# The order in which two lanes' steps are merged on each engine, and the numbers of constant products, laid out once more in a chain of eight attention and feed-forward stages

## Chip, cores and metric

One core of one Trainium2 chip. The metric is the device time of one execution in microseconds.

## What is computed

32 samples of 128 tokens by 128 features go through four layers, each a gated cross-attention and a gated feed-forward, in fp32:

```
x = x + tanh(g_xattn[l]) * attention_l(norm(x), ctx)
x = x + tanh(g_ffn[l])   * ffn_l(norm(x))
```

- Layer 0: attention with 16 heads of 8; a mixture of 8 experts, top 2, and 2 shared ones.
- Layer 1: causal attention with 16 heads; a "switched" attention as feed-forward: 8 value and output experts for each head, top 2 chosen by a token's own gates on the value side and on the output side.
- Layer 2: an mLSTM (4 heads, exponential gates, cumulated logarithms of the forget gates); a feed-forward of ternary weights with a convolution of width 3 in between.
- Layer 3: a wide attention with 16 heads and a feed-forward of its own; a mixture of 16 experts.

## The kernel before

The weights stay in SBUF. The samples are worked in 8 turns (counted from 0) of 2 lanes of 2 samples (G = 2). A lane goes through eight stages in each turn: A0 (small attention), M0 (mixture), A1 (small attention), SW (switched attention), ML (mLSTM), CF (feed-forward with convolution), WA (wide attention), M3 (second mixture). Every engine runs both lanes, so that one lane has work where the other waits.

What each engine does for a lane is written as a generator (pe_lane, act_lane, dve_lane, pool_lane, sp_lane) that yields between its steps ("chunks"). On each engine weave() (line 135) merges the two generators into one stream of instructions: a chunk n of a turn t of lane k has the number t * TURN + BEATS[k][n], and the chunk with the lower number is issued first. The numbers do nothing else; the waits on semaphores stay within the chunks. Each turn of a lane has 173 chunks on TensorE and 22 on SyncE. Engines run in order, so a chunk whose semaphore is not up holds the other lane's chunks behind it.

```
while heads:
    head = min(heads, key=lambda h: h[:2])
    ...
    turn, chunk = divmod(n + 1, len(beats[k]))
    head[0], head[2] = turn * TURN + beats[k][chunk], n + 1
```

spare() (line 334) issues so many products of a constant bf16 identity (L336), into a bank that is written afterwards anyway, as the next number in SPARES says: 101 calls a lane and turn, each ahead of a wait of TensorE. Their results are used by nobody.

The lines that the prediction goes by:

- SyncE, sp_lane: for each lane the switched attention stores its values to DRAM and reloads them in another layout: pv_d (store L1784, load L1788), the mixing matrix mix_d (store L1792, load L1795), v_d (store L1800, load L1804), the selection sel_d (L1807, L1810) and the outputs o_d (store L1816, load L1819), one for each sample, in 22 chunks with a wait each. The inputs of the next turn and the output of this are chunks 20 and 21.
- ScalarE: spread (L949) makes the mixing weights from what mix_d's load brought; keep_values (L954) takes the mixed values out of PSUM for v_d; L942 spreads q and k; L862 and L869 are the attentions' exponentials and copies.
- TensorE: L344 turns the normed x; L408, L431 and L440 end a small attention; L532, L535 and L544 are the projections of the switched attention, L559 its scores, L574 its mixed values, L589 its attention's product with the values, L603 and L616 its outputs; L685 and L693 are in the mLSTM.
- VectorE: L1202 takes the maximum of scores; L1369 finishes the mixing matrix that mix_d's store waits for.

Of the kernel before, what the change touches and what calls it, by code (L numbers as in the profile page):

```python
# [49 lines left out]
), (  # L50
# [11 lines left out]
))  # L62
BEATS_ACT = ((
# [7 lines left out]
), (  # L71
# [7 lines left out]
))  # L79
BEATS_DVE = ((  # L80
# [10 lines left out]
), (  # L91
# [10 lines left out]
))  # L102
BEATS_POOL = ((
    47832, 55688, 59143, 64674, 67070, 70207, 71015, 77823, 79861, 83113, 84484,
# [1827 lines left out]
```

## Time and profile before

| what | us |
|---|---|
| median of three runs (lowest, highest) | 2446.69 (2446.49, 2448.3) |
| the profiled execution | 2447.47 |
| its span, first to last instruction | 2445.4 |
| TensorE busy | 2223.2 |
| VectorE busy | 1749.4 |
| ScalarE busy | 1290.7 |
| mean granted clock of TensorE | 0.976 |

The profiled execution is 0.8 us above the median; 2.1 us of it lie outside the span. Busy shares add up over stages with different limits, so the table alone does not say what holds a stage: the rows below do, by stretch.

### The profile page before, as it was taken

Reading aid. Unit: us, or ns where it says so; the run is one execution under the profiler, and the core shown is the slowest. Engines: PE = TensorE matmul, PEld = TensorE weight load, DVE = VectorE, ACT = ScalarE, POOL = GpSimd, SP = SyncE. Lnnn points to the kernel's source line nnn. Section 1 sums busy time; section 2 is a strip of 40 time slices with the busy share of each in tenths; the row PEclk is TensorE's granted clock in tenths of the full one; section 3 lists DMA queues with packets and bytes.
Section 4 is the critical chain, followed back from the end, with each engine's and each line's share of the span. In section 5 each row is a group of like instructions: output and inputs, shape, how many; then the busy total and the mean of one; then the engine's idle time right before and its main releaser. Section 6 shows DMA issues by size and latency. Waiting matters only on the chain.

```text
span 2445.4 us, 51545 instructions
## 1 busy us (share of the span) xinstructions
PE 2223.2 (91%) x19938; PEld 1612.2 (66%) x19938; DVE 1749.4 (72%) x5567; ACT 1290.7 (53%) x3714; POOL 141.2 (6%) x180
## 2 busy tenths in 40 slices
PE   7899989989899998999899988999889998899998
PEld 3668657676567765677666766667666676666766
DVE  6874787757877577774877758777587775877657
ACT  4366354664547545474444744547344473445734
POOL 0000100001000010000100010000110001100010
PEclk9999999999999899998999999999899998999989
DMA  4034000340004300042000520006100061000610
GB/s 172 1 88 104 9 14 1 96 96 10 14 1 113 79 9 14 1 122 70 9 14 1 129 63 9 14 1 147 45 18 6 2 156 36 20 3 13 151 29 5
DMA packets 312516, 115.52 MB, mean 47 GB/s; under 512 B 268752, under 2 KB 295376, under 8 KB 312016
## 3 DMA queue, kind: packets, MB, share of 16 engines
q1 hardware_dynamic: 312272, 112.23, 17.9%
q8 instruction: 158, 2.59, 0.4%
q14 instruction: 86, 0.70, 0.1%
HBM read 63.96 MB, written 48.23 MB: 46 GB/s over the span
## 4 chain that ended last, share of the span: by engine, by line
PE 49%; DVE 30%; ACT 8%; DMA 5%; issue 4%; POOL 3%; SPq 1%; DVEq 0%; ACTq 0%
PE banks L450 7%; PE banks L386 6%; PE banks L589 3%; PE banks L505 3%; ACT PP L862 3%; PE banks L616 3%; PE banks L383 2%; PE banks L336 2%; DVE nm L1202 2%; DVE qk L1283 2%; DMA mix_d<-gs 2%; PE banks L544 2%; PE banks L397 2%; PE banks L559 2%; POOL mv L1741 2%
## 5 line engine op out<-in xcount | busy, mean ns | idle before, releaser
L862 ACT ACTIVATE PP<-banks,nm 128x128 f32<-128x128 f32 x1568 | 443.7, 391 | 210.8 <-DVE nm L1202 120.5
L1202 DVE TENSOR_REDUCE nm<-banks 128x4 f32<-128x512 f32 (+1 forms) x400 | 261.3, 675 | 136.3 <-PE banks L386 100.7
L336 PE MATMUL banks<-identb 128*128 128x256 bf16 x1840 | 289.1, 277 | 16.4 <-ACT PP L1017 8.5
L450 PE MATMUL banks<-w_sb,PP 128*128 128x128 f32 x1536 | 247.8, 285 | 45.7 <-ACT PP L862 17.6
L450 PEld LDWEIGHTS banks<-w_sb,PP 128*128 128x128 f32 x1536 | 167.4, 142 | 122.9 <-issue 64.0
L336 PEld LDWEIGHTS banks<-identb 128*128 128x128 bf16 x1840 | 177.2, 101 | 106.6 <-issue 48.0
L1741 POOL TENSOR_TENSOR mv<-mv,half 128x2 f32<-128x2 f32 x160 | 113.0, 706 | 2135.0 <-DVE mv L1099 2135.0
L1245 DVE COPY PP<-banks 128x512 f32<-128x512 f32 x256 | 175.8, 689 | 61.1 <-PE banks L450 60.2
L505 PE MATMUL banks<-w_sb,qk 128*128 128x128 f32 x1280 | 180.6, 280 | 2.0 <-DVE qk L1346 1.3
L505 PEld LDWEIGHTS banks<-w_sb,qk 128*128 128x128 f32 x1280 | 164.7, 194 | 20.1 <-issue 11.4
L386 PE MATMUL banks<-qk,gs 32*128 32x512 f32 x512 | 147.5, 653 | 0.0
L589 PE MATMUL banks<-va,PP 128*128 128x128 f32 x1024 | 139.3, 282 | 2.3 <-DVE oa L1391 2.3
L589 PEld LDWEIGHTS banks<-va,PP 128*128 128x128 f32 x1024 | 124.6, 194 | 8.5 <-DVE oa L1391 4.2
L853 ACT ACTIVATE xnT<-banks 128x256 f32<-128x256 f32 x128 | 49.1, 384 | 149.0 <-PE banks L344 149.0
L544 PE MATMUL banks<-xnT,w_sb 128*128 128x256 f32 x512 | 121.0, 384 | 0.6
L916 ACT ACTIVATE tmp<-banks 128x256 f32<-128x256 f32 x160 | 60.5, 383 | 103.1 <-PE banks L475 102.3
L544 PEld LDWEIGHTS banks<-xnT,w_sb 128*128 128x128 f32 x512 | 94.0, 190 | 25.4 <-issue 7.7
L397 PE MATMUL banks<-PP,va 128*32 128x128 f32 x2048 | 102.8, 284 | 3.9 <-DVE PP L1245 3.9
L1346 DVE TENSOR_TENSOR qk<-qk,banks 128x256 f32<-128x256 f32 x256 | 96.2, 416 | 8.2 <-PE banks L498 4.4
L1114 DVE TENSOR_SCALAR xn<-x,mv 128x128 f32<-128x128 f32 x256 | 76.7, 342 | 34.0 <-POOL mv L1741 32.6
L474 PE MATMUL banks<-xnT,w_sb 128*128 128x256 f32 x320 | 97.9, 388 | 0.5 <-DVE wstat L1700 0.5
L475 PE MATMUL banks<-xnT,w_sb 128*128 128x256 f32 x320 | 95.6, 381 | 0.0
(283 smaller groups left out, 4267.4 us busy)
## 6 DMA issues: line engine op xcount, KB each, us to landing
va<-v_d SPq DMA_DIRECT2D x32, 512.0 KB, 3.8
o_d<-oa SPq DMA_DIRECT2D x64, 256.0 KB, 4.2
va<-o_d SPq DMA_DIRECT2D x32, 512.0 KB, 4.4
pv_d<-PP SPq DMA_DIRECT2D x32, 256.0 KB, 2.0
oa<-pv_d SPq DMA_DIRECT2D x32, 256.0 KB, 3.2
v_d<-PP SPq DMA_DIRECT2D x16, 512.0 KB, 4.0
v_d<-tmp SPq DMA_DIRECT2D x16, 512.0 KB, 4.4
w_sb<-weights SPq DMA_DIRECT2D x1, 5599.0 KB, 24.2
```

The costliest lines, as they stand in the source:

```text
L336: pe.matmul(bank(k, n)[:, cols(c, T)], identb[:, :], bc(identb[:, :], 1, G), start=True, stop=True, skip_group_check=True)
L386: pe.matmul(bank(k, c), qT[k][rows, cols(b)], km[rows, b, :], start=False, stop=True, skip_group_check=True).then_inc(s_ps[k], 1)
L397: e = pe.matmul(bank(k, 3)[32 * j:32 * j + 32, cols(g)], v4[:, b, HQ * g + j, :], PT[k][:, 512 * (u % 2) + 128 * j:][:, 0:128], start=True ...
L450: e = pe.transpose(bank(k, 2)[:, cols(j)], P[k][:, 512 * (u % 2) + 128 * j:][:, 0:128], ident)
L474: pe.matmul(hb[:, 0:T], w("w1_0", n * 128, (n + 1) * 128), xnT[k][:, :], start=True, stop=True)
L505: e = pe.matmul(bank(k, 0)[:, cols(b)], qk[k][:, n * T + b * 128:n * T + (b + 1) * 128], w(weight, n * 128, (n + 1) * 128), start=n == 8 a ...
L544: pe.matmul(bank(k, n % 4)[:, 0:T], w(("sq1", "sk1")[n % 2], n // 2 * 128, (n // 2 + 1) * 128), xnT[k][:, :], start=True, stop=True).then_ ...
L589: e = pe.matmul(bank(k, 3)[:, cols(j)], PT[k][:, 512 * (u % 2) + 128 * j:][:, 0:128], va3[k][:, n:G * H + 1:G * H - n, :], start=True, sto ...
L862: e = act.activation(P[k][:, 512 * (u % 2) + 128 * j:][:, 0:128], bank_[:, cols(j)], ACT.Exp, bias=nm[k][:, m:m + 1])
L1202: e = dve.tensor_reduce(m, b3(scores[:, 0:maps * 128], maps), AX.X, ALU.max, negate=True)
L1245: dve.tensor_copy(PT[k][:, cols(n % 2, 512)], bank(k, 2)).then_inc(pT_ok[k], 1)
L1741: pool.tensor_tensor(a, a, half[:, 0:n], ALU.pow).then_inc(pw[k], 1)
```

## The change

Only the numbers in BEATS_PE, BEATS_ACT, BEATS_DVE, BEATS_POOL and BEATS_SP, and in SPARES, are others. TURN stays at 39873. No instruction but the constant products is added or removed.

```diff
 BEATS_PE = ((
-    -1250, -612, -326, -44, 358, 653, 679, 1059, 1283, 1395, 1454, 1561, 1923, 2116, 2199, 2211, 2316, 2889, 2917, 2958,
...
+    0, 468, 605, 752, 1234, 1691, 1757, 2193, 2482, 2548, 2703, 2769, 3076, 3291, 3570, 3618, 3684, 4085, 4462, 4528, 4653,
...
 BEATS_SP = ((
-    -242752, -242553, -242553, -238131, -238131, -237804, -237804, -237058, -236981, -233923, -230618, -221598, -219346,
-    -218796, -217615, -212325, -212215, -209270, -206607, -206485, -203699, -203699,
+    16795, 16911, 17360, 17410, 17765, 17815, 17945, 18356, 18920, 19533, 20031, 20850, 21669, 22414, 22463, 22704, 23055,
+    23779, 24239, 24662, 36199, 39918,
 ), (
-    -235003, -231213, -230164, -229008, -229008, -228143, -225901, -221262, -221262, -221262, -221262, -218853, -213790,
-    -209157, -209065, -206564, -205345, -205168, -204765, -204680, -203168, -203066,
+    18840, 19064, 19405, 19455, 19810, 19860, 19953, 20364, 20693, 21228, 21390, 22209, 23145, 23730, 24298, 24539, 24890,
+    24980, 25641, 26064, 39969, 57767,
 ))
...
 SPARES = (
-    3, 1, 0, 0, 1, 0, 0, 0, 0, 0, 0, 0, 0, 0, 0, 0, 0, 0, 0, 1, 7, 0, 8, 0, 3, 0, 0, 0, 0, 0, 0, 0, 0, 0, 0, 0, 4, 0, 0, 0,
-    0, 0, 0, 0, 0, 2, 1, 0, 5, 0, 0, 1, 5, 0, 0, 0, 0, 0, 0, 0, 0, 0, 0, 0, 0, 0, 0, 0, 0, 0, 1, 0, 0, 0, 0, 2, 1, 3, 8, 3,
-    0, 9, 8, 0, 0, 0, 3, 0, 0, 2, 2, 3, 4, 0, 3, 8, 0, 9, 3, 1, 0,
+    7, 0, 0, 0, 1, 0, 0, 0, 2, 0, 0, 0, 0, 0, 0, 1, 0, 0, 0, 1, 1, 0, 11, 0, 2, 0, 1, 0, 0, 0, 0, 0, 5, 0, 0, 0, 1, 0, 0, 0,
+    0, 0, 0, 0, 0, 1, 0, 0, 3, 0, 3, 0, 2, 3, 0, 0, 0, 0, 0, 0, 0, 0, 0, 0, 0, 0, 3, 0, 0, 0, 3, 0, 0, 0, 0, 0, 2, 3, 7, 2,
+    0, 7, 4, 0, 0, 0, 7, 0, 0, 1, 3, 0, 3, 0, 2, 9, 0, 3, 5, 8, 0,
 )
```

Merging both sets of numbers by weave()'s rule gives these orders (lane.chunk):

- SyncE, one turn, before: 0.20 0.21 1.20 1.21 0.0 to 0.8, 1.0, 0.9, 1.1, 0.10, 1.2 to 1.6, 0.11, 1.7 to 1.10, 0.12, 1.11, 0.13, 0.14, 1.12, 0.15, 0.16, 0.17, 1.13, 1.14, 0.18, 1.15, 0.19, 1.16 to 1.19 (the first four are of the turn before). After: 0.20 0.21 1.20 0.0 to 0.5, 1.21, 0.6, 0.7, 1.0, 0.8, 1.1, 1.2, 1.3, 0.9, 1.4, 1.5, 1.6, 0.10, 1.7, 1.8, 0.11, 1.9, 1.10, 0.12, 1.11, 0.13 to 0.16, 1.12, 1.13, 0.17, 0.18, 1.14, 1.15, 0.19, 1.16 to 1.19. Chunks 0 and 1 are pv_d's stores; 2, 3, 4 are pv_d's load, mix_d's store and load for sample 0, 5, 6, 7 for sample 1; 8 and 9 are v_d's store and load for sample 0, 10 and 11 for sample 1.
- TensorE, in the switched attention: lane 1's last four chunks of the small attention before it and its first (81 to 84) move by one to three steps of lane 0: 81 from ahead of 0.85 to behind 0.88, 82 to ahead of 0.95, 83 to ahead of 0.96; 1.84 goes ahead of 0.103; 0.124 ahead of 1.118. Elsewhere ten places a turn where one to three neighbouring chunks of the two lanes change places.
- ScalarE: twelve such places a turn.
- VectorE: the same order, but for the first chunks of turn 0, where lane 0's first six now come ahead of lane 1's first three. GpSimd: the same order.
- SPARES adds up to 117 instead of 115 for a lane and turn: 1872 products instead of 1840.

## Rows read from the trace of the kernel before

**Rows 1.** The page, busy time of each engine (share of the span), instructions
```profile
PE 2223.2 (91%) x19938; PEld 1612.2 (66%) x19938; DVE 1749.4 (72%) x5567; ACT 1290.7 (53%) x3714; POOL 141.2 (6%) x180
```
**Rows 2.** The page, the chain that ended last: shares of the span by engine
```profile
PE 49%; DVE 30%; ACT 8%; DMA 5%; issue 4%; POOL 3%; SPq 1%; DVEq 0%; ACTq 0%
```
**Rows 3.** Busy time by stretch, turns 3 and 4: length, busy, PEclk, DMA share, GB/s
```profile
926.60:1227.70 301.10, 276.97 (x2495) 201.82 (x2495) 216.93 (x692) 161.06 (x464) 17.62 (x22) 0.97 0.17 44
1227.70:1526.40 298.70, 272.36 (x2495) 197.91 (x2493) 216.75 (x691) 161.07 (x464) 17.62 (x22) 0.99 0.18 44
```
**Rows 4.** The same view, first mixture and second small attention of turn 3
```profile
950.00:1000.00 50.00, 47.55 (x367) 34.29 (x365) 41.48 (x130) 22.69 (x71) 1.39 (x2) 1.00 0.00 1
1000.00:1044.00 44.00, 41.30 (x332) 25.24 (x331) 31.19 (x71) 23.59 (x77) 1.40 (x2) 1.00 0.00 1
```
**Rows 5.** Timeline of TensorE, turn 3: start, us, group, xcount
```profile
1060.38 1.16 PE L559 MATMUL banks<-qk 64*128 64x128 f32 x16
```
**Rows 6.** The same timeline, constant products of the mLSTM, with the idle time before
```profile
1153.11 1.05 PE L336 MATMUL banks<-identb 128*128 128x256 bf16 x8 [0.50 <-ACT PP L1017]
```
**Rows 7.** The same timeline, the last mixture
```profile
1220.08 0.27 PE L487 MATMUL banks<-identb,gpart 128*128 128x128 bf16 x2 [2.31 <-DVE gpart L1332]
```
**Rows 8.** Line L949 over the whole run: its idle time, who waited for it (us, times)
```profile
  DMA gt<-mix_d: 25.6, 18
...
  PE banks L574: 20.7, 17
```
**Rows 9.** The chain in order of time, turn 3: start, us, what
```profile
1070.84 0.37 SPq L1800
1071.25 2.33 SPq L1788
1073.63 2.86 DMA mix_d<-gs
...
1077.53 2.93 DMA mix_d<-gs
1080.48 2.77 DMA gt<-mix_d
```
**Rows 10.** Timeline of VectorE, switched attention of turn 3
```profile
1063.32 0.68 DVE L1202 TENSOR_REDUCE nm<-banks 128x4 f32<-128x512 f32 x1
...
1070.26 0.38 DVE L1369 SCALAR_TENSOR_TENSOR gs<-gt,gm 128x128 f32<-128x128 f32 x1
...
1075.03 0.38 DVE L1369 SCALAR_TENSOR_TENSOR gs<-gt,gm 128x128 f32<-128x128 f32 x1
```
**Rows 11.** Timeline of SyncE's transfers as issued, the same stretch: start, us of issue
```profile
1056.04 0.32 SPq L1792 DMA_DIRECT2D mix_d<-gs  x1
1057.57 0.37 SPq L1795 DMA_DIRECT2D gt<-mix_d  x1
...
1078.15 0.43 SPq L1804 DMA_DIRECT2D va<-v_d  x1
```
**Rows 12.** Timeline of ScalarE, the same stretch
```profile
1075.76 1.68 ACT L942 ACTIVATE qk<-banks 128x256 f32<-128x256 f32 x5
1078.62 1.28 ACT L949 ACTIVATE mixd<-gt,w_sb 128x128 f32<-128x128 f32 x4 [1.18 <-DMA gt<-mix_d]
```
**Rows 13.** The chain in order of time, end of the switched attention of turn 3
```profile
1109.84 2.35 DMA o_d<-oa
...
1112.20 4.96 DMA va<-o_d
```
**Rows 14.** Waits, 1060 to 1090: engine line, waited for: us, times, longest
```profile
ACT mixd L949 <- DMA gt<-mix_d: 2.3, 2, 1.2
```
**Rows 15.** Busy time by stretch, mLSTM of turns 3 and 4, columns as in Rows 3
```profile
1127.50:1150.50 23.00, 20.36 (x196) 15.28 (x193) 11.06 (x39) 11.29 (x24) 2.45 (x2) 0.75 0.00 1
...
1428.80:1451.80 23.00, 18.63 (x194) 13.13 (x194) 13.46 (x48) 12.28 (x28) 2.71 (x3) 0.93 0.00 1
...
1145.90:1152.70 6.80, 5.12 (x10) 1.93 (x9) 5.67 (x23) 0.79 (x4) 1.75 (x1) 0.50 0.00 0
```
**Rows 16.** Timeline of TensorE, start of turn 0
```profile
12.78 0.69 PE L344 MATMUL banks<-w_sb,xn 128*128 128x128 f32 x2 [1.36 <-DVE xn L1114]
```

More of the change, by code:

```diff
@@ L38 @@
 BEATS_PE = ((
[11 rows of a table removed]
-), (
[11 rows of a table removed]
[11 rows of a table added]
+), (
[11 rows of a table added]
 ))
 BEATS_ACT = ((
[7 rows of a table removed]
-), (
[7 rows of a table removed]
[7 rows of a table added]
+), (
[7 rows of a table added]
 ))
 BEATS_DVE = ((
[10 rows of a table removed]
-), (
[10 rows of a table removed]
[10 rows of a table added]
+), (
[10 rows of a table added]
 ))
 BEATS_POOL = ((
-    47832, 55688, 59143, 64674, 67070, 70207, 71015, 77823, 79861, 83113, 84484,
+    214, 5981, 10413, 16065, 26017, 29072, 29644, 32766, 34383, 35940, 36339,
 ), (
-    48901, 58347, 63494, 64749, 70006, 73170, 76144, 78979, 81361, 86183, 87523,
+    1732, 7515, 11905, 18081, 27516, 30656, 31164, 33820, 35566, 36711, 37341,
 ))
 BEATS_SP = ((
-    -242752, -242553, -242553, -238131, -238131, -237804, -237804, -237058, -236981, -233923, -230618, -221598, -219346,
-    -218796, -217615, -212325, -212215, -209270, -206607, -206485, -203699, -203699,
-), (
-    -235003, -231213, -230164, -229008, -229008, -228143, -225901, -221262, -221262, -221262, -221262, -218853, -213790,
-    -209157, -209065, -206564, -205345, -205168, -204765, -204680, -203168, -203066,
+    16795, 16911, 17360, 17410, 17765, 17815, 17945, 18356, 18920, 19533, 20031, 20850, 21669, 22414, 22463, 22704, 23055,
+    23779, 24239, 24662, 36199, 39918,
+), (
+    18840, 19064, 19405, 19455, 19810, 19860, 19953, 20364, 20693, 21228, 21390, 22209, 23145, 23730, 24298, 24539, 24890,
+    24980, 25641, 26064, 39969, 57767,
 ))
 SPARES = (
[3 rows of a table removed]
[3 rows of a table added]
 )
```

110 rows, old and new, of tables (BEATS_ACT, BEATS_DVE, BEATS_PE) are left out of this document.

## Prediction, made before the changed kernel had run

> **What bounds the kernel now.** I read the page from the top: busy time by engine, then the chain of work that ended last, then the stretches. TensorE is busy 2223.2 of 2445.4 us, VectorE 1749.4 [rows 1], but neither share says what a change of order is worth. The chain does: 49% TensorE, 30% VectorE, 8% ScalarE, 5% DMA, 4% issue, 3% GpSimd [rows 2]. No instruction becomes cheaper here, so only the DMA, issue and waiting parts, and TensorE's clock, can give or take time. Then the turns. Turn 3 of the eight (counted from 0) lasts 301.1 us and turn 4 298.7, with as good as the same busy time of VectorE (216.93 and 216.75) and ScalarE (161.06 and 161.07) [rows 3]. What differs from turn to turn is the granted clock and the transfers.
>
> **Stages where the order is worth nothing.** The order on VectorE is the same before and after but at the start of turn 0, and on GpSimd it is the same everywhere. In the first mixture and its neighbour TensorE works 47.55 of 50 us and VectorE 41.48; in the second attention TensorE 41.30 of 44 [rows 4]. The two hand over to one another in turn, and both lanes are ready there, so a swap of two neighbouring steps of about 1 us each moves who waits, not the end. For the swaps outside the switched attention, some ten places a turn on TensorE and ten on ScalarE, I take 0. Bounds: one step of 1.1 us (16 products of L559 [rows 5]) wrongly put ahead of the needed one, once a turn, either way: plus or minus 1.1 x 8 = 9 us. I take the middle because each such swap has its mirror a few steps later and the stages stay as full as they are.
>
> **Constant products.** The counts rise from 115 to 117 for each lane and turn, so 16 x 2 = 32 more. Eight in a row take 1.05 us, of which the last drains 0.27, so one costs 0.11 us [rows 6]. All 32 on the path: 3.5 us; hidden in front of waits, as the 1840 of now nearly all are: 0. Most of what moves goes ahead of waits that exist (to the last call of the wide mixture, in front of a wait of 2.31 us on gpart, eight instead of one [rows 7]). I take 0.1 us a turn.
>
> **The switched attention, where the gain is.** This stage has transfers through DRAM that come back before the work can go on, all issued by SyncE in one order for both lanes. Over the whole run ScalarE waits 25.6 us, 18 times, at L949 for the mixing matrix to come back from mix_d, and TensorE then 20.7 us behind it at L574 [rows 8]: some 3.2 and 2.6 us in each of eight turns. In turn 3 the chain goes: 1070.84 issue of a store of v_d (L1800), 1071.25 the load of pv_d, whose issue took 2.33 us behind that store, 1073.63 store of mix_d in flight 2.86, 1077.53 the next one 2.93, 1080.48 the load 2.77, and then ScalarE goes on [rows 9]. SyncE stood in front of that v_d store because lane 0's values were ready only at 1070.8 (the ACTIVATE of L954 that ended then), and lane 1's transfers were queued behind it, though lane 1's first mix matrix was ready at 1070.64 (L1369, 1070.26 + 0.38) and its second at 1075.41 [rows 10]. In the new order the v_d store of lane 0's second sample stands behind both mix_d stores of lane 1 and just ahead of lane 1's second mix_d load.
>
> What that gives, step by step. Lane 1's load of pv_d then waits only for its own store, long issued: it goes at about 1069.5. The mix_d store goes when its matrix is ready, 1070.65 + 0.4 = 1071.06 rather than 1073.63. It lands by one of two rows: with a quiet queue 1.5 us later (1056.04 issued, the load behind it could go at 1057.57), with a busy one 2.9 [rows 9, 11]: 1072.6 to 1073.9, against 1076.48. The load then goes and lands at 1075 to 1076, and ScalarE's L949 is no longer held by it until 1078.62 but by its own work, which ends at 1077.4 to 1077.6 (five activations of L942 from 1075.76 took 1.68) [rows 12]: 1.0 us earlier, and so is TensorE's L574. The second mix_d store is ready at 1075.41 and no longer has the late load ahead: issued 1075.83 instead of 1077.53, landing 1077.4 to 1078.7, and the second load lands 2.77 later, 1080.2 to 1081.5 instead of 1083.26. ScalarE has the first spread and L954 until 1081.1, so the second spread starts at 1081.1 to 1081.5: 1.8 to 2.2 earlier. From there the stage is ScalarE and TensorE in turn, then VectorE, and then two transfers (2.35 and 4.96 us [rows 13]) that start when the last of that is done; they all shift with it. So 2.0 us in turn 3. The mean wait of [rows 8] is 3.2 a turn against 2.3 in turn 3 [rows 14], so 2.0 is not the best turn. Bounds: 0.8 (the first wait alone, less 0.2) and 3.1.
>
> What it costs. Three steps of lane 1's end of the second attention (L408, L431, L440: 4, 2 and 4 products, 1.2 us in all) and one of L344 move into lane 0's projections (L544). Lane 0's first scores, done at 1061.54 now (L559, 1060.38 + 1.16 [rows 5]), end at 1062.8. VectorE reads them at 1063.32 [rows 10], so the 1.2 is hidden with 0.5 to spare; without that cover it would be 1.2 x 8 = 10 us. Lane 0's second v_d store goes some 6 us later and its reload at about 1081.5 instead of 1078.15 [rows 11], landing near 1086; it is lane 0's second sample, whose first product (L589) comes after four calls of the first sample's, behind 1095. At the end of the stage two stores of o_d of lane 1 go behind one of lane 0 that waits for VectorE until 1109.84 [rows 13]; lane 1's reload then lands up to 1.6 us later, and it had 2 to spare. I take 0.05 a turn for all of it, and up to 0.6 as the bound.
>
> The Trainium skill, page "DMA: Bandwidth & Descriptors", section on the anatomy of one DMA, has a fixed part of about 2.0 us in every DMA, most of it completion. By that figure alone the two mix_d stores would land at 1073.1 and 1077.8, in the middle of the bounds above, and the sum would be the same to 0.1 us a turn. In this trace it is 1.5 quiet and 2.9 busy.
>
> **TensorE's clock in the mLSTM.** In six of eight turns the granted clock of the stretch about the mLSTM's start is down (0.75 in turn 3), in turns 1 and 4 it is up (0.93 in turn 4) [rows 15]. Turn 4 is 2.4 us shorter than turn 3 [rows 3], and this is where: two stretches of turn 3 such as 1145.9 to 1152.7 stand at 0.50, 1.2 GHz [rows 15]. One such pair a turn costs some 2.5. The change takes constant products out of five calls of this stage (9 to 7, 8 to 4, 8 to 7, 3 to 2, 2 to 0) and puts some into three (0 to 3, 1 to 3, 1 to 2): 28 a lane instead of 32, with those for the second lane's waits cut most. I take no change: six turns low as now. Bounds: two more turns (+5) or none low (-15).
>
> **Start.** VectorE's order in turn 0 puts lane 0 first: lane 0's normalised x, for which TensorE now idles until 12.78 [rows 16], is ready about 2.8 us earlier. But seven constant products of lane 1's first call then lie ahead of lane 0's next step at 0.21 each, twice the 0.11, as the clock is at half there. Net -0.3, bounds -3 and +3.
>
> **Sum.** 8 x (-2.0 + 0.1 + 0.05) = -14.8, -0.3 for the start: -15.1. The profiled execution took 2447.47 us with a span of 2445.4, so 2.1 lie around it, and these stay; the median of the three runs is 0.8 under it. 2446.7 - 15.1 = 2431.6 us.
>
> **Rivals.**
> 1. *Slower: the clock falls oftener.* Price: 2.5 us for each turn and low pair. Mechanism: fewer constant products ahead of the mLSTM's waits (9 to 7, 8 to 4, 2 to 0) leave TensorE idle for longer, the clock drops, and the products behind it, which are on the path there, run at half speed. For it: TensorE is busy only 5.12 of 6.8 us in such a stretch [rows 15], it already happens in six turns, and the calls lose four products a lane. Against it: turns 1 and 4 show the same program without. The pair in turns 1 and 4 as well, and one more pair in each turn, in the convolution behind it: 10 x 2.5 = +25: 2446.7 - 15 + 25 = 2456 us. It decides from the sixth further pair on, where the gain of 15 is gone. The Trainium skill, page "TensorE: Matmul & The Clock Gate", Part 1, says that the gate follows how busy the array has recently been, which would make fewer constant products a loss; its remark that the phase is free-running speaks for a result that shifts from turn to turn, as [rows 15] show.
> 2. *No gain: the transfers land as late as before,* as lane 0's store of v_d and its reload, 512 KB each, are in flight from 1067.8 on beside lane 1's small ones, or the 1.2 us in the projections is not hidden. Then -2.0 becomes -0.5 to 0: 2443 to 2448, say 2445.
> 3. *More gain: the low pairs vanish,* because the stage now starts elsewhere, or the second wait in the worse turns gives all its 3.1: -15 more at most: 2417 us.
> 4. *The change doesn't do what it says* (order as good as kept): out, as merging the new numbers by the rule gives other orders on TensorE, ScalarE and SyncE.
>
> **Chances.** Forecast 0.47, rival 1 0.24, rival 2 0.15, rival 3 0.14. About 0.2% (4.9 us) is what a measurement of this kernel can tell from no change. Faster by more: forecast and rival 3, 0.61. Within it: 0.15. Slower: 0.24. The range takes in the bounds of the switched attention (-0.8 to -3.1 a turn, 2440 to 2422), of the swaps (9 either way) and of the clock, and reaches to the near parts of both outer rivals: 2413 to 2455. The likeliest case alone: 2424 to 2440.
>
> **What would show it.** After: ScalarE's wait at L949 for mix_d well under 25.6 us, that of TensorE at L574 with it; turn length down 2 us in every turn, the DMA share of the chain from 5% to about 4%; the clock of the mLSTM stretch as in [rows 15] in six turns. It is wrong if the wait at L949 falls and the turn doesn't (then the next wait, for o_d, took it), if the clock drops in stretches that were at 1.0, or if VectorE waits at L1202 for scores.

## The result, and the profile of the kernel after

The changed kernel takes 2433.95 us (median of 8 runs, 2429.59 to 2442.25) against 2447.38 (8 runs, 2444.34 to 2453.34): ratio 0.9945, 95% interval 0.9928 to 0.9962. That is 13.4 us less; 15.1 were forecast.

| what | before | after |
|---|---|---|
| median, us | 2447.38 | 2433.95 |
| span of the profiled execution | 2445.4 | 2430.4 |
| TensorE busy | 2223.2 | 2219.7 |
| VectorE busy | 1749.4 | 1748.1 |
| ScalarE busy | 1290.7 | 1295.1 |
| mean granted clock | 0.976 | 0.978 |

The page of the kernel after, busy time of each engine, the chain by engine, and the group of constant products:

```profile
PE 2219.7 (91%) x19954; PEld 1602.0 (66%) x19970; DVE 1748.1 (72%) x5567; ACT 1295.1 (53%) x3714; POOL 141.2 (6%) x180
...
PE 43%; DVE 36%; ACT 8%; issue 5%; DMA 4%; POOL 3%; SPq 1%; DVEq 0%; ACTq 0%
...
L336 PE MATMUL banks<-identb 128*128 128x256 bf16 x1872 | 298.1, 278 | 15.0 <-DVE identb L1653 5.2
```

The DMA share of the chain is down from 5% to 4% [rows 2], as the prediction wanted. The idle time and the waiters of L949 over the whole run, after:

```profile
  DMA gt<-mix_d: 11.9, 12
...
  PE banks L574: 12.2, 12
```

ScalarE waits 11.9 us for mix_d instead of 25.6, TensorE behind it 12.2 instead of 20.7 [rows 8]. So far this is the forecast's picture. But where the time went doesn't fit it. Busy time by stretch of the kernel after (length, PE, PEld, DVE, ACT, POOL busy, PEclk, DMA share, GB/s), for turn 0, turns 3 and 4, and turn 7:

```profile
5.20:316.60 311.40, 279.12 (x2449) 199.35 (x2452) 225.13 (x716) 161.45 (x463) 17.65 (x22) 0.97 0.24 71
...
919.50:1219.20 299.70, 275.53 (x2497) 198.64 (x2497) 216.71 (x691) 161.61 (x464) 17.62 (x22) 0.98 0.18 44
1219.20:1519.60 300.40, 276.64 (x2497) 199.71 (x2498) 216.75 (x691) 161.60 (x464) 17.62 (x22) 0.98 0.18 44
...
2121.10:2427.50 306.40, 281.57 (x2544) 204.23 (x2544) 220.00 (x699) 162.11 (x465) 17.62 (x22) 0.98 0.17 42
```

and of the kernel before, turns 0 and 7:

```profile
4.90:325.90 321.00, 287.09 (x2444) 202.89 (x2445) 224.82 (x711) 161.11 (x463) 17.66 (x22) 0.96 0.23 69
2132.10:2442.50 310.40, 284.50 (x2545) 207.94 (x2543) 221.24 (x703) 161.65 (x465) 17.62 (x22) 0.97 0.17 41
```

Turn 0 is 9.6 us shorter and turn 7 4.0; turns 1 to 6 together went from 1806.2 (325.9 to 2132.1) to 1804.5 (316.6 to 2121.1), 1.7 us, where six times 1.85, some 11, were forecast. A wait at L949 that falls while the turn doesn't is the prediction's own first sign of being wrong. Of these six, turn 1 got 2.2 longer (301.8 against 299.6) and turn 4 1.7 (300.4 against 298.7 in [rows 3]), the two that had their clock up before; the other four are 5.6 shorter together. Each of these lengths is of one execution. They suggest that something gives time at the start, and that something takes it back in the turns. The mean granted clock over the whole run did not fall (0.976 and 0.978). The start first: timeline of VectorE after, the maxima of scores (L1202) of turn 0,

```profile
15.53 0.69 DVE L1202 TENSOR_REDUCE nm<-banks 128x4 f32<-128x512 f32 x1 [5.99 <-PE banks L386]
...
18.32 0.69 DVE L1202 TENSOR_REDUCE nm<-banks 128x4 f32<-128x512 f32 x1
...
24.43 0.69 DVE L1202 TENSOR_REDUCE nm<-banks 128x4 f32<-128x512 f32 x1
...
27.08 0.68 DVE L1202 TENSOR_REDUCE nm<-banks 128x4 f32<-128x512 f32 x1
```

and before:

```profile
18.71 0.69 DVE L1202 TENSOR_REDUCE nm<-banks 128x4 f32<-128x512 f32 x1 [5.47 <-PE banks L386]
19.99 0.68 DVE L1202 TENSOR_REDUCE nm<-banks 128x4 f32<-128x512 f32 x1
...
26.75 0.69 DVE L1202 TENSOR_REDUCE nm<-banks 128x4 f32<-128x512 f32 x1 [1.17 <-PE banks L386]
...
29.40 0.68 DVE L1202 TENSOR_REDUCE nm<-banks 128x4 f32<-128x512 f32 x1
```

The first is 3.2 us earlier. Then, in the switched attention of turn 3, the chain in order of time after:

```profile
1062.92 4.43 DMA mix_d<-gs
...
1068.41 2.86 DMA mix_d<-gs
1071.29 2.76 DMA gt<-mix_d
```

and SyncE's transfers as they are issued, just before and behind the first of these stores:

```profile
1059.65 0.43 SPq L1800 DMA_DIRECT2D v_d<-PP  x1
1060.92 1.35 SPq L1784 DMA_DIRECT2D pv_d<-PP  x1
1062.31 0.49 SPq L1788 DMA_DIRECT2D oa<-pv_d  x1
1062.92 0.93 SPq L1792 DMA_DIRECT2D mix_d<-gs  x1
1064.39 0.83 SPq L1804 DMA_DIRECT2D va<-v_d  x1
```

Counted from the start of the turn (926.6 before, 919.5 after), lane 1's first mix_d store is issued at 143.4 instead of 147.0 [rows 9]: 3.6 us earlier. But it is in flight 4.43 us instead of 2.86, with a store of v_d (512 KB), a store of pv_d (256) and a load of pv_d (256) issued within 3.3 us ahead of it, and a load of v_d (512) behind it. The second one is issued at 148.9 instead of 150.9 and flies as long as before.

### The profile page after: what moved, and what is told of

The parts are those of the page before. It is cut to its first block, busy times and chain, and to the rows that moved or that the text cites. A ratio compares the mean times of both kernels' runs of the same rounds, so it can differ in the third digit from the quotient of the medians.

```text
span 2430.4 us, 51561 instructions
## 1 busy us (share of the span) xinstructions
PE 2219.7 (91%) x19954; PEld 1602.0 (66%) x19970; DVE 1748.1 (72%) x5567; ACT 1295.1 (53%) x3714; POOL 141.2 (6%) x180
## 4 chain that ended last, share of the span: by engine, by line
PE 43%; DVE 36%; ACT 8%; issue 5%; DMA 4%; POOL 3%; SPq 1%; DVEq 0%; ACTq 0%
PE banks L450 7%; PE banks L386 5%; PE banks L589 3%; PE banks L505 3%; PE banks L616 3%; DVE qk L1283 2%; DVE nm L1202 2%; ACT PP L862 2%; POOL mv L1741 2%; PE banks L383 2%; DMA mix_d<-gs 2%; DVE tmp L1281 2%; DVE xn L1114 2%; PE banks L397 2%; DVE PP L1245 2%
## 5 line engine op out<-in xcount | busy, mean ns | idle before, releaser
L1202 DVE TENSOR_REDUCE nm<-banks 128x4 f32<-128x512 f32 (+1 forms) x400 | 261.3, 675 | 123.1 <-PE banks L386 97.7
L336 PE MATMUL banks<-identb 128*128 128x256 bf16 x1872 | 298.1, 278 | 15.0 <-DVE identb L1653 5.2
L336 PEld LDWEIGHTS banks<-identb 128*128 128x128 bf16 x1872 | 179.2, 101 | 92.3 <-issue 36.5
L386 PE MATMUL banks<-qk,gs 32*128 32x512 f32 x512 | 145.8, 646 | 0.0
L853 ACT ACTIVATE xnT<-banks 128x256 f32<-128x256 f32 x128 | 49.3, 385 | 166.5 <-PE banks L344 166.5
L544 PE MATMUL banks<-xnT,w_sb 128*128 128x256 f32 x512 | 122.7, 382 | 0.4
L474 PE MATMUL banks<-xnT,w_sb 128*128 128x256 f32 x320 | 99.4, 393 | 0.6 <-DVE wstat L1700 0.5
L829 PE MATMUL banks<-xnT,w_sb 128*128 128x256 f32 x320 | 86.5, 399 | 10.4 <-ACT qk L1080 9.7
```

Of the source, the lines that this page charges most:

```text
L336: pe.matmul(bank(k, n)[:, cols(c, T)], identb[:, :], bc(identb[:, :], 1, G), start=True, stop=True, skip_group_check=True)
L386: pe.matmul(bank(k, c), qT[k][rows, cols(b)], km[rows, b, :], start=False, stop=True, skip_group_check=True).then_inc(s_ps[k], 1)
L544: pe.matmul(bank(k, n % 4)[:, 0:T], w(("sq1", "sk1")[n % 2], n // 2 * 128, (n // 2 + 1) * 128), xnT[k][:, :], start=True, stop=True).then_ ...
L1202: e = dve.tensor_reduce(m, b3(scores[:, 0:maps * 128], maps), AX.X, ALU.max, negate=True)
```

## Experiments

All times below are medians. Each ratio is to runs of the kernel before on the same chip in the same session; those spread by 19 to 25 us there, so that the ratios carry the comparisons, and 0.1% is 2.4 us. A ratio is not the quotient of the medians and can differ from it by 0.1 to 0.2%, which matters for the small effects. The first four runs ask which part of the change holds the gain.

**The start alone.** One argument for weave gives the first places; the tables stay.

```diff
-def weave(beats, lanes):
+def weave(beats, lanes, first=()):
...
-        head = min(heads, key=lambda h: h[:2])
+        head = heads[first.pop(0)] if first else min(heads, key=lambda h: h[:2])
...
-            weave(BEATS_PE, (pe_lane(pe, 0), pe_lane(pe, 1)))
+            weave(BEATS_PE, (pe_lane(pe, 0), pe_lane(pe, 1)), (0, 0, 0, 0, 0, 1))
...
-            weave(BEATS_DVE, (dve_lane(dve, 0), dve_lane(dve, 1)))
+            weave(BEATS_DVE, (dve_lane(dve, 0), dve_lane(dve, 1)), (0, 0, 0, 0, 0, 0, 1, 1, 1))
```

> The kernel before, with the new order only at the very start of turn 0: lane 0's first chunks ahead of lane 1's on VectorE (nine places) and on TensorE (six places); all numbers and counts as before. By the prediction the start is worth 0.3 us, so 2447 us, ratio 1.000. By the rival theory, read from the trace of the changed kernel (its turn 0 reached turn 1's start 9.6 us earlier, about 6 of it before the first mixture), the start alone gives 4 to 6 us: 2442, ratio 0.998.

Measured: 2442.38 us, ratio 0.9971 (0.9952 to 0.9990), so 7 us less with an interval of 2 to 12; by the medians of the session (2445.88 before) it is 3.5. Busy time by stretch, before and then this run, both from 20 to 36.5 us:

```profile
20.00:36.50 16.50, 14.20 (x53) 5.95 (x53) 9.71 (x21) 8.52 (x30) 0.00 (x0) 1.00 0.52 224
```

```profile
20.00:36.50 16.50, 13.54 (x91) 6.80 (x89) 15.28 (x37) 8.95 (x30) 0.70 (x1) 1.00 0.51 219
```

VectorE does 15.28 us of work in a stretch in which it did 9.71, and TensorE starts 91 products instead of 53 in less busy time. The same pair of products of L383 shows why, timeline of TensorE before and then in this run:

```profile
23.65 1.06 PE L383 MATMUL banks<-mb,identb 128*128 128x512 bf16 x2
...
30.64 2.08 PE L386 MATMUL banks<-qk,gs 32*128 32x512 f32 x4
```

```profile
20.00 1.06 PE L360 MATMUL banks<-w_sb,ctxT 128*128 128x128 f32 x4
...
21.71 0.71 PE L383 MATMUL banks<-mb,identb 128*128 128x512 bf16 x2
22.34 1.13 PE L386 MATMUL banks<-qk,gs 32*128 32x512 f32 x4
```

Four products of L386 take 1.13 at 22.3 us here; before they took 2.08 as late as 30.64. TensorE came to 2.4 GHz some 15 us earlier in this execution (the PEclk column says 1.00 in both, it misses the half speed of the start). It is not the chance of one execution: the second group of L386, at 22 to 24 us, takes 1.13 in eleven of the twelve kept traces with the new start and 1.54 in the twelfth, and in the only two with the old one (the kernel before and SyncE's order alone) the groups take 2.08 until 29 to 31 us. So the start gives more than a shift by the 3.2 us by which its order leads. The rival holds in its direction; of its size the interval says only 2 to 12.

**SyncE's order alone,** and **the change without it.** Only the block BEATS_SP is exchanged, in the kernel before and in the kernel after.

```diff
 BEATS_SP = ((
-    -242752, -242553, -242553, -238131, -238131, -237804, -237804, -237058, -236981, -233923, -230618, -221598, -219346,
...
+    16795, 16911, 17360, 17410, 17765, 17815, 17945, 18356, 18920, 19533, 20031, 20850, 21669, 22414, 22463, 22704, 23055,
...
```

> The kernel before with the new numbers for SyncE alone. By the prediction all of the gain in the switched attention comes from this order: ScalarE's wait at L949 for mix_d falls from 25.6 to about 12 us, each turn is 2 us shorter, 2431 us, ratio 0.994. By the rival theory the wait falls but half of it comes back in later waits and the rest of the gain was the start's: 2440 us, ratio 0.997.

> The kernel after with SyncE's old numbers. By the prediction the gain is gone but for the start: 2446 us. By the rival theory some 6 us of the start stay: 2440 to 2442 us, and the wait at L949 is back at 25 us.

Measured: SyncE's order alone 2431.60 us, ratio 0.9922 (0.9895 to 0.9949, so 12 to 26 us less); the change without it 2454.08 us, ratio 1.0025 (1.0009 to 1.0042). L949 over the whole run, SyncE's order alone (its profiled execution, 2421.70 us, is the fastest of its six):

```profile
  DMA gt<-mix_d: 15.6, 13
...
  PE banks L574: 12.2, 12
```

and the change without it:

```profile
  DMA gt<-mix_d: 33.2, 16
...
  PE banks L574: 25.0, 11
```

Both sides agree: SyncE's order is worth 0.8%, 19 us, taken alone and again 0.8% (1.0025 - 0.9945), 20 us, taken from the change. The place of the gain is as predicted; the forecast 16 us lie within the interval. The rest of the change, with the start in it, makes the kernel slower than before. As the start gives some 7 us, there must be some 13 of loss in counts and orders, if the parts add up.

**Two of TensorE's chunks put back.** In the kernel after, lane 1's chunks 81 and 84 (of 190 a lane and turn, not 173); 82 and 83, which moved further, stay:

```diff
-    15489, 15677, 15830, 15878, 15956, 16004, 16148, 16968, 17416, 17510, 18207, 18477, 18838, 18896, 19148, 19206, 19264,
+    15489, 15677, 15830, 15878, 15956, 16004, 16148, 16300, 17416, 17510, 18400, 18477, 18838, 18896, 19148, 19206, 19264,
```

> The kernel after with two of TensorE's chunks put back: lane 1's last turn_out (L408) ahead of lane 0's projections, and lane 1's transpose of the normed x (L344) behind lane 0's first mixed values (L574). In the changed kernel's trace lane 1's projections (L535) start 0.58 us later against the stage's start than before. If these two moves are what costs, and the cost is on the path (against the prediction, which had it hidden), each turn is 0.5 us shorter: 2430 us against the changed kernel's 2434. If hidden, as predicted: no change, 2434.

Measured: 2435.43 us, ratio 0.9947 (0.9928 to 0.9965) against the changed kernel's 0.9945. No difference: these two moves are hidden, as predicted, and not what costs.

**SyncE's order and the start, the rest as before**: both edits above in the kernel before. **The same with the new counts**: SPARES of the change as well.

> The kernel before with the new numbers for SyncE and the new order at the very start of turn 0 on VectorE and TensorE; TensorE's and ScalarE's orders otherwise, and the counts of constant products, as before. If the two gains add and everything else of the change gives nothing or costs (theory from the first runs: SyncE -12 us in the switched attention, the start -5, the rest of the change +3 to +8), this beats the changed kernel: about 2428 us, ratio 0.992. If the rest of the change was worth something by itself, it is slower than the changed kernel: 2437 or more.

> As the run before, with the new counts of constant products too. What then separates it from the changed kernel is the order on TensorE and ScalarE alone. If the counts cost (32 products more a run, four fewer a lane in the mLSTM's calls), this is 3 to 5 us slower than without them and the mLSTM's stretch is at half clock in seven or eight turns instead of about four; if they are neutral, the same within 2 us.

Measured: 2422.86 us, ratio 0.9900 (0.9874 to 0.9925), by ratio 11 us less than the changed kernel; and with the counts 2430.36, ratio 0.9936 (0.9912 to 0.9960). The two gains add (0.9922 x 0.9971 = 0.9893), and the new counts cost 0.36%, 9 us (7.5 by the medians; every execution with the new counts is slower than every one with the old). 32 products of 0.11 us would be 3.5.

**The change with the old counts**, and **the change with ScalarE's old order**: the block SPARES, or BEATS_ACT, of before in the kernel after.

> The kernel after with the old counts of constant products. If the new counts cost, it is 3 to 5 us faster than the changed kernel (2430); if the orders on TensorE and ScalarE cost, it is as slow as the changed kernel, 2434, and its stretch from lane 0's last scores to its first outputs (L559 to L603) stays 0.6 us longer than before the change.

> The kernel after with ScalarE's old order. By the prediction ScalarE's twelve swaps a turn are worth nothing: 2434 us like the changed kernel. If they are what costs 0.6 us a turn on VectorE ahead of the last divisions of the switched attention, 2429.

Measured: old counts 2431.91 us, ratio 0.9942 (0.9924 to 0.9959), the changed kernel's own ratio; ScalarE's old order 2453.64 us, ratio 1.0030 (1.0011 to 1.0049). The first seems to speak against the run before; the last experiment takes it up. It says one thing more. From SyncE's order and the start (0.9900) to this kernel (0.9942), both of the same session and with the old counts, only the orders of TensorE and ScalarE differ, and they cost 0.42%, 10 us: the slowest execution of the one, 2425.24, is faster than the fastest of the other, 2428.06. With the new counts the same step costs nothing that can be told (0.9936 to 0.9945). So counts and orders each cost 9 or 10 us alone, and together no more than one of them. The second is a surprise: ScalarE's order is worth 0.85%, 21 us, under TensorE's new order. A wait of VectorE and the timeline of ScalarE, switched attention of turn 3, with ScalarE's old order:

```profile
DVE tp L1152 <- ACT gs L931: 4.2, 1, 4.2
...
1063.53 1.02 ACT L954 ACTIVATE PP<-banks 128x1024 f32<-128x1024 f32 x1 [1.86 <-PE banks L574]
1064.44 0.38 ACT L853 ACTIVATE xnT<-banks 128x256 f32<-128x256 f32 x1
```

and in the changed kernel:

```profile
DVE tp L1152 <- ACT gs L931: 2.7, 1, 2.7
...
1055.64 0.38 ACT L853 ACTIVATE xnT<-banks 128x256 f32<-128x256 f32 x1 [1.08 <-PE banks L344]
1056.76 1.02 ACT L954 ACTIVATE PP<-banks 128x1024 f32<-128x1024 f32 x1 [0.74 <-PE banks L574]
```

VectorE waits 1.5 us longer for lane 1's first projections with the old order. ScalarE has lane 1's copy of the normed x (L853) behind lane 0's L954 there, which waits 1.86 us for the products of L574. TensorE's new order has issued lane 1's L344 ahead of those products, so that L853 could go first, as it does in the changed kernel. If it is so in every turn, 1.5 x 8 = 12 of the 20 us lie there. TensorE's new order needs ScalarE's with it.

**The calls of the mLSTM.** In the kernel with SyncE's order and the start's, the new counts in the eight calls that the change alters from the end of the switched attention through the mLSTM (the expectations call them nine), and then the complement: all new counts but those.

```diff
-    0, 0, 0, 0, 0, 2, 1, 0, 5, 0, 0, 1, 5, 0, 0, 0, 0, 0, 0, 0, 0, 0, 0, 0, 0, 0, 0, 0, 0, 0, 1, 0, 0, 0, 0, 2, 1, 3, 8, 3,
-    0, 9, 8, 0, 0, 0, 3, 0, 0, 2, 2, 3, 4, 0, 3, 8, 0, 9, 3, 1, 0,
+    0, 0, 0, 0, 0, 2, 1, 0, 5, 0, 0, 1, 5, 0, 0, 0, 0, 0, 0, 0, 0, 0, 0, 0, 0, 0, 3, 0, 0, 0, 3, 0, 0, 0, 0, 0, 2, 3, 7, 2,
+    0, 7, 4, 0, 0, 0, 3, 0, 0, 2, 2, 3, 4, 0, 3, 8, 0, 9, 3, 1, 0,
```

> The fastest kernel so far (SyncE's new order and the start's, counts as before) with the new counts of constant products in the nine calls of the end of the switched attention and the mLSTM alone (0 to 3, 1 to 3, 2 to 0, 1 to 2, 8 to 7, 3 to 2, 9 to 7, 8 to 4). If these are what costs in the run with all new counts (whose mLSTM stretch never fell under 39.6 us, where it is 38.0 or 40.6 with the old ones), it is 5 to 8 us slower: 2429, and its stretch is 39.5 to 41 in every turn. If the clock's phase is all there is to it, no difference: 2423.

> The complement: all the other new counts, the old ones in those nine calls. If the mLSTM's calls are what costs, it stays at 2423 and the stretch is 38.0 or 40.6; if the products added elsewhere cost, 2426 to 2430.

Measured: new counts in these calls 2432.91 us, ratio 0.9929 (0.9905 to 0.9953); in all the others 2422.78 us, ratio 0.9886 (0.9862 to 0.9909). The two differ by 0.43%, 10 us; against the kernel with all old counts, 0.9900 in the session before, these calls cost 0.29%, 7 us, though they hold four products fewer a lane and turn (28 for 32). The added products elsewhere cost nothing that these runs tell. Busy time by stretch, 198 to 224 us after the start of turns 3 to 6, first with the new counts in these calls (the clock is the third column from the end):

```profile
1117.90:1143.90 26.00, 22.21 (x205) 16.53 (x204) 11.30 (x39) 12.08 (x27) 2.44 (x2) 0.76 0.07 16
1419.10:1445.10 26.00, 22.63 (x225) 16.91 (x220) 11.50 (x41) 12.09 (x27) 2.45 (x2) 0.81 0.05 12
1720.40:1746.40 26.00, 22.48 (x225) 16.52 (x222) 11.16 (x39) 12.08 (x27) 2.18 (x2) 0.80 0.07 14
2022.10:2048.10 26.00, 22.11 (x202) 15.85 (x202) 13.40 (x48) 12.81 (x30) 2.64 (x3) 0.80 0.00 1
```

and with the old ones there:

```profile
1108.80:1134.80 26.00, 22.41 (x240) 16.06 (x240) 13.11 (x45) 12.23 (x28) 2.64 (x3) 0.89 0.09 19
1408.40:1434.40 26.00, 21.92 (x244) 16.42 (x244) 12.49 (x46) 13.01 (x29) 3.14 (x3) 0.91 0.10 21
1709.00:1735.00 26.00, 23.13 (x228) 17.55 (x223) 10.91 (x40) 12.08 (x27) 2.45 (x2) 0.77 0.05 11
2010.20:2036.20 26.00, 23.18 (x206) 16.18 (x206) 12.82 (x43) 12.07 (x28) 2.45 (x2) 0.76 0.00 1
```

With the old counts some turns keep the clock up (0.89, 0.91), with the new ones none does. The same view over turns 1 to 7 of the other runs with SyncE's new order: with these new counts 0.75 to 0.85 in the changed kernel and 0.74 to 0.82 in the one with the start and all new counts; with the old ones 0.87 or more in four of seven turns with SyncE's order alone and in three with the start as well. But the time does not follow this clock. The changed kernel with all old counts has 0.87 in four of seven turns and is no faster for it, and the change without SyncE's order has 0.82 to 0.87 in five turns, new counts and all, and is slower than the kernel before. Nor does the clock over the whole run: its median over all executions is 0.9815 with the old counts in these calls and 0.975 with the new ones, but 0.977 both with the start and all old counts and with the start and all new ones, which are 7.5 to 9 us apart. So these counts cost time and mostly go with a lower clock in this stretch; that the clock is the way by which they cost it is not shown. What the clock does to one operation, timeline of TensorE in turn 3, new counts (at half clock) and then old (at full):

```profile
1124.47 3.68 PE L616 MATMUL banks<-w_sb,tmp 64*64 64x128 f32 x32 [0.64 <-ACT tmp L961]
```

```profile
1115.84 1.98 PE L616 MATMUL banks<-w_sb,tmp 64*64 64x128 f32 x32 [0.71 <-ACT tmp L961]
```

**More products instead of fewer.** In the kernel with SyncE's order and the start's, 14 products instead of 1 for lane 1 in front of the wait of 1.58 us for L1440:

```diff
-        spares = [itertools.cycle(SPARES) for _ in range(LANES)]
+        spares = [itertools.cycle(SPARES[:76] + (n,) + SPARES[77:]) for n in (1, 14)]
```

> The fastest kernel so far with 14 constant products instead of 1, for lane 1 alone, ahead of the mLSTM's first cumulated sums (L684), where TensorE idles 1.58 us for VectorE (L1440). If the low clock of the mLSTM lasts because TensorE idles there, the second low stretch of the pair gets shorter or goes, and it is worth up to 1 us a turn: 2416 to 2420. If not, 13 more products at half clock last 2.8 us against 1.6 of idle and it is 1 us a turn slower in the low turns: 2426 to 2432.

Measured: 2432.16 us, ratio 0.9927 (0.9899 to 0.9954), 7 us slower by ratio than the kernel it is built on and 9 by the medians, though those are of two sessions. Timeline of TensorE, turn 3:

```profile
1136.46 2.87 PE L336 MATMUL banks<-identb 128*128 128x256 bf16 x14
1139.16 0.38 PE L684 MATMUL banks<-causb,identb 128*128 128x512 bf16 x1
1139.38 1.02 PE L685 MATMUL banks<-tmp,ones 128*128 128x512 f32 x2
```

The clock did come back in this turn: L685 takes 1.02 for its pair here, where it takes 1.91 in the kernel without them. But the fourteen products last 2.87 us, mostly at half clock, in a gap of 1.58. Saved and spent about balance in a low turn; of turns 1 to 7 one has 0.93 in the stretch and one 0.87, the others 0.80. The trade is bad.

**The change with the old counts in these calls only:** the two lines of the diff above, backwards, in the kernel after.

> The kernel after with the old counts of constant products in the nine calls of the end of the switched attention and the mLSTM, and nothing else put back. If those counts cost the whole change what they cost in the runs without its orders on TensorE and ScalarE (0.4%), it is about 8 us faster than the changed kernel: 2425, ratio 0.991, with its mLSTM stretch at 38.0 or 40.6 us. If under the new orders they cost nothing (as the run with all old counts suggests, 0.9942 against 0.9945), it stays at 2432 to 2434.

Measured: 2427.98 us, ratio 0.9908 (0.9880 to 0.9937), 0.37% better than the changed kernel, though the intervals overlap and only one of its turns 1 to 7 has the clock at 0.87. With all counts old it had been 0.9942. So under the change's own orders these calls would cost what they cost elsewhere, and the other new counts would give about as much (0.9942 to 0.9908): taken back together, the two would cancel, which would be why the run with all old counts showed nothing. With overlapping intervals this is a reading and not shown, and the clock does not bear it out: this kernel has a clock of 0.87 in one turn and the slower one with all old counts in four.

## Why the prediction was right, and where it was not

**The total** was forecast at 2431.6 us, and 2433.95 was measured. The change of -13.4 stands against -15.1. It came so near by luck: the start gave some 7 us where 0.3 was forecast, and counts and orders took back 11 (0.9900 to 0.9945) where 1 was, two errors of opposite sign.

**What bounds the kernel; L949 and SyncE's queue: right.** The wait for mix_d behaved as read from [rows 8] to [rows 12], and two experiments put 19 to 20 us on SyncE's order (12 to 26 for the one taken alone) where 16 were forecast. Its inner step was mis-sized. The mix_d store was to fly 1.5 to 2.9 us; it flew 4.43 in turn 3, as it now goes out among transfers of 256 and 512 KB (the rival of the transfers that land as late as before, in part). The fixed 2.0 us that the prediction quotes from the Trainium skill, page "DMA: Bandwidth & Descriptors", anatomy of one DMA, are fitted there to transfers that GpSimd issues; SyncE's store of mix_d took between 1.5 and 4.43. TensorE's wait at L574 fell by 8.5 us in all, 1.1 a turn, not 2.0. What brings SyncE's order to 19 beyond that is open. In its profiled run three of turns 1 to 7 kept the clock of the mLSTM at 0.90 to 0.93, where the kernel before had two, and its turn 0 was shorter as well; but that is its fastest execution, and over all of them the median clock is 0.974 against 0.973 before.

**"It lands by one of two rows" was the wrong kind of bound:** both rows are of the order of before, and the new order makes a third state.

**The costs in the switched attention: hidden, as far as tried.** With two of the four moved steps put back nothing changed (0.9947 against 0.9945). VectorE's wait for the scores at L1202, named as a sign of being wrong, did not grow there (2.6 us before in 30 us of turn 3, 1.9 after).

**The swaps elsewhere, 0: right in sum only.** From the kernel with all new counts, SyncE's order and the start's (0.9936) to the change (0.9945) the orders of TensorE and ScalarE together give or cost nothing that can be told. With the old counts the same orders cost 10 us (0.9900 to 0.9942), the outer edge of the prediction's bound of 9. And TensorE's without ScalarE's costs 0.85%. So "each swap has its mirror" was no reason for a 0: what a swap is worth hangs on the other engine's order and on the counts.

**The start, -0.3 with bounds of 3: wrong.** It is -7 (-2 to -12; -3.5 by the medians). The step netted the earlier x against seven constant products at half clock, and took the later course as given. In fact what ran at half clock until 36 us runs at full clock from about 22.

**Constant products, 0.1 us a turn, and the clock "no change": wrong.** The new counts cost 9 us in TensorE's and ScalarE's old orders, 7 to 10 of them in the mLSTM's calls; in the new orders all of them together cost nothing (0.9942 with the old ones, 0.9945 with the new). The first rival had the place and the sign: fewer products in the mLSTM's calls, a loss. Its mechanism, more turns at half clock, is borne out in part. Turn 4's loss, 298.7 to 300.4 us, fits it: it had its clock up before (0.93 in [rows 15]) and at 0.75 in the longer stretch after. But the clock over the whole run did not fall, and two kernels that differ in the counts alone, 0.9900 and 0.9936, have the same one (0.977). Its chance of 0.24 was for a net loss; as a part of the sum it should have been in the forecast, since the counts that I listed went down in five of eight calls. The page "TensorE: Matmul & The Clock Gate" of the Trainium skill, Part 1, has the gate follow the array's recent activity; the clock in the mLSTM's stretch agrees (at most 0.85 in any turn of the kernels with these new counts and SyncE's new order, up to 0.93 with the old ones), the times agree only in part. Which of the calls does it, and why the three that have more (0 to 3, 1 to 3, 1 to 2) do not help, was not separated: their own products lie on the path too.

**What would show it:** the wait and the DMA share did, "turn length down 2 us in every turn" did not. The lengths, turn by turn, led to both wrong terms.

The fastest kernels here are the old one with SyncE's new order and the new start, 2422.86 us, and the same with the new counts outside the mLSTM's calls, 2422.78: by ratio 11 to 14 us below the changed kernel.

## What to carry to other kernels

Where an order is laid out anew as a whole, judge it by parts that can be exchanged alone, and look at each turn's length before the total: here gains of some 19 and 7 us and a loss of about 11 looked like one gain of 13. Don't expect the parts to add up, either: counts and orders cost 9 and 10 us one by one and 11 together. Orders of two engines that hand over to each other are one edit. A queue that every lane shares should hold no transfer that waits on one lane in front of another lane's ready one; and the number of constant products is to be tried stage by stage, not counted over the whole kernel.

## What the runs showed of the hardware that I had not expected

- The same 64 KB store of mix_d was in flight 1.5 us alone [rows 11], 2.86 behind a store of v_d and a load of pv_d [rows 9], and 4.43 behind three such transfers and ahead of a fourth.
- TensorE reached full clock at 21 to 24 us in all twelve traces with the new start and at 34 to 37 in the two with the old one, though lane 0's first products lead by 3 us only: four products of L386 took 1.13 at 22.34 and 2.08 at 30.64.
- Other counts in eight calls, four constant products fewer a lane and turn in sum, made the kernel 0.3 to 0.4% slower; which of the calls does it is open.
